# Linear-attention layers: the query feature's minimum on GpSimd, and the attention's last step as one VectorE operation per quarter of the channels

## What is computed

```python
def _feature_map(x):
    return jax.nn.elu(x) + 1.0
for i in range(B):                       # B = 8 layers
    residual = x
    Q = _feature_map(jnp.einsum('nsd,hdk->nshk', x, Wq[i]) + bq[i])
    Kf = _feature_map(jnp.einsum('nsd,hdk->nshk', x, Wk[i]) + bk[i])
    V = jnp.einsum('nsd,hdk->nshk', x, Wv[i]) + bv[i]
    KV = jnp.sum(Kf * V, axis=1)
    sumK = jnp.sum(Kf, axis=1)
    Z = 1.0 / (Q * sumK[:, None] + 1e-06)
    att = Q * KV[:, None] * Z
    att = att.reshape(n, s, H * K)
    y = jax.nn.gelu(att @ Wo[i] + bo[i])
    x = _layer_norm(y + residual, ln1_s[i], ln1_b[i])
    residual = x
    h = jax.nn.gelu(x @ W1[i] + b1[i])
    h = jax.nn.gelu(h @ W2[i] + b2[i])
    x = _layer_norm(h + residual, ln2_s[i], ln2_b[i])
```

## Time and profile before

| what | value |
|---|---|
| median of 3 runs | 3349.62 us (3346.64 to 3351.68) |
| the profiled execution | 3358.28 us |
| its span | 3356.5 us |
| TensorE busy | 2989.0 us, 89% of the span |
| VectorE busy | 2665.6 us, 79% |
| ScalarE busy | 2443.9 us, 73% |
| GpSimd busy | 843.9 us, 25% |
| mean granted TensorE clock | 0.944 |

### The profile page before, as it was taken

How to read it: one execution, slowest core, us unless ns; L and a number is a source line. 1 busy time by engine, 2 the same in 40 slices (tenths; PEclk the granted TensorE clock), 3 DMA queues, 4 the chain that set the end, 5 groups by cost and what they waited for, 6 DMA issues and landing times. The chain is left out here.

```text
span 3356.5 us, 51221 instructions
## 1 busy us (share of the span) xinstructions
PE 2989.0 (89%) x14363; PEld 1985.1 (59%) x14368; DVE 2665.6 (79%) x10483; ACT 2443.9 (73%) x4542; POOL 843.9 (25%) x1000
## 2 busy tenths in 40 slices
PE   6999998172599999999999999999999999999767
PEld 5777776161456666666666666666666666666444
DVE  4656665753489999988999999899999999898647
ACT  5888886031478888888888888788888888888643
POOL 2444444283111121111112112112111211121126
PEclk9999998586699999999999999999999999999868
DMA  1000000222100000000000000000000000000000
GB/s 54 1 0 0 0 0 14 100 34 38 64 1 1 20 13 1 20 7 8 1 25 8 1 20 7 8 12 15 7 1 20 13 1 1 1 1 1 1 7 26
DMA packets 31563, 46.34 MB, mean 14 GB/s; under 512 B 5315, under 2 KB 21731, under 8 KB 31334
## 3 DMA queue, kind: packets, MB, share of 16 engines
q1 hardware_dynamic: 25702, 39.46, 3.5%
q0 software_dynamic: 5632, 4.20, 0.9%
HBM read 35.16 MB, written 8.49 MB: 13 GB/s over the span
## 5 line engine op out<-in xcount | busy, mean ns | idle before, releaser
L1774 DVE TENSOR_SCALAR t_feat_q<-t_recip,t_neg_mean 128x256 f32<-128x256 f32 x1024 | 400.8, 453 | 112.4 <-ACT t_recip L1634 109.4
L1480 PE MATMUL t_o_ps<-t_feat_q,t_wo 128*128 128x512 f32 x1024 | 474.5, 596 | 6.8 <-issue 4.1
L1626 ACT ACTIVATE t_recip<-t_feat_q,t_z_scale 128x256 f32<-128x256 f32 x1024 | 434.8, 499 | 1.7 <-DVE t_feat_q L1774 1.0
L1612 ACT ACTIVATE t_exp_k<-t_k_ps 128x1024 f32<-128x1024 f32 x256 | 259.8, 1015 | 233.4 <-PE t_k_ps L1457 233.4
L1737 DVE CUSTOM_DVE_ANT_0 t_junk<-t_v_ps,t_feat_k 128x256 f32<-128x256 f32 x1024 | 390.7, 419 | 8.2 <-PE t_v_ps L1457 8.0
L1727 DVE SCALAR_TENSOR_TENSOR t_feat_k<-t_exp_k,t_k_ps 128x256 f32<-128x256 f32 x1024 | 369.4, 417 | 21.4 <-ACT t_exp_k L1612 21.4
L1898 POOL TENSOR_TENSOR t_var_eps<-t_moments,t_ln_eps 128x4 f32<-128x4 f32 x128 | 69.3, 542 | 1240.2 <-DVE t_moments L1785 1240.2
L1616 ACT ACTIVATE t_exp_q<-t_q_ps 128x1024 f32<-128x1024 f32 x256 | 261.7, 1022 | 87.1 <-PE t_q_ps L1457 86.3
L1763 DVE SCALAR_TENSOR_TENSOR t_feat_q<-t_exp_q,t_q_ps 128x1024 f32<-128x1024 f32 x256 | 312.7, 1222 | 8.8
L1480 PEld LDWEIGHTS t_o_ps<-t_feat_q,t_wo 128*128 128x128 f32 x1024 | 194.5, 190 | 180.9 <-issue 160.0
L243 POOL TENSOR_TENSOR a_probs<-a_probs,a_inv 128x256 f32<-128x256 f32 (+1 forms) x256 | 209.3, 839 | 274.5 <-DVE a_inv L340 274.5
(11 more groups left out here) (370 smaller groups left out, 7424.5 us busy)
## 6 DMA issues: line engine op xcount, KB each, us to landing
t_raw_w<-in_wk SPq DMA_DIRECT2D x8, 512.0 KB, 3.7
t_raw_w<-in_wq SPq DMA_DIRECT2D x8, 512.0 KB, 4.6
t_raw_w<-in_wv SPq DMA_DIRECT2D x8, 512.0 KB, 5.4
t_raw_o<-in_wo SPq DMA_DIRECT2D x8, 512.0 KB, 3.7
t_raw<-in_w SPq DMA_DIRECT2D x16, 256.0 KB, 2.7
x<-in_x SPq DMA_DIRECT2D x4, 512.0 KB, 6.9
tokens_dram<-r_hn SPq DMA_DIRECT2D x8, 256.0 KB, 2.3
e_w_raw<-in_fc_w SPq DMA_DIRECT2D x4, 512.0 KB, 3.8
```

Of the source, the lines that this page charges most:

```text
L1480: last = pe.matmul(o_ps[:], wo[:, chunk, :], feat_q[:, s, chunk, :], start=(chunk == 0), stop=(chunk == NC - 1), skip_group_check=True)
L1612: act.activation(exp_k[:], k_ps[:], ACT.Exp, bias=-1.0).then_inc(c["k_exp"], 1)
L1626: last = act.activation(recip[:, q % 2, k * UNIT + n * SEQ:k * UNIT + (n + 1) * SEQ], feat_q[:, s, chunk, cols], ACT.Ln, bias=1.0, scale=z ...
L1774: last = dve.tensor_scalar(feat_q[:, s, chunk, cols], recip[:, q % 2, k * UNIT + n * SEQ:k * UNIT + (n + 1) * SEQ], -1.0, neg_mean[:, s, n ...
```

## The change

The minimum of the query feature goes from VectorE to GpSimd (`less_one`): the carrier waits for the exponential, the minimum follows and raises `q_less_one`, for which VectorE's feature waits as before. The four calls of a step stand between GpSimd's other work. The attention's last step becomes one operation over a quarter of the channels, which are two chunks for two batches: it reads `recip` and, as a second tensor, `neg_mean` spread over the 256 tokens; for that `neg_mean` is laid out with the batch innermost.

```diff
-        neg_mean = sb("t_neg_mean", [P, 2, 2, NC])
+        neg_mean = sb("t_neg_mean", [P, 2, NC, 2])
...
-                dve.scalar_tensor_tensor(neg_mean[:, s, :, :], kv_all[:], -1.0, inv_sum[:], ALU.mult, ALU.mult).then_inc(c["kv_ready"], 1)
+                dve.scalar_tensor_tensor(neg_mean[:, s, :, :].rearrange("p c n -> p n c"), kv_all[:], -1.0, inv_sum[:], ALU.mult, ALU.mult).then_inc(c["kv_ready"], 1)
 
             def feature_q(t, s, q):
-                dve.wait_ge(c["q_exp"], 4 * t + q + 2)
-                dve.tensor_scalar(exp_q[:], exp_q[:], 1.0, -1.0, ALU.min, ALU.add).then_inc(c["q_less_one"], 1)
                 dve.wait_ge(c["q_less_one"], 4 * t + q + 2)
...
-                for k in range(2):
-                    for n in range(2):
-                        chunk, cols = 2 * q + k, slice(n * SEQ, (n + 1) * SEQ)
-                        last = dve.tensor_scalar(feat_q[:, s, chunk, cols], recip[:, q % 2, k * UNIT + n * SEQ:k * UNIT + (n + 1) * SEQ],
-                                                 -1.0, neg_mean[:, s, n, chunk:chunk + 1], ALU.add, ALU.mult)
-                last.then_inc(c["att_ready"], 1)
+                means = neg_mean[:, s, 2 * q:2 * q + 2, :].rearrange("p c n -> p (c n)").unsqueeze(2).broadcast_to([P, 4, SEQ])
+                dve.scalar_tensor_tensor(feat_q[:, s, 2 * q:2 * q + 2, :].rearrange("p c (n t) -> p (c n) t", n=2),
+                                         recip[:, q % 2, :].rearrange("p (a t) -> p a t", t=SEQ), -1.0, means,
+                                         ALU.add, ALU.mult).then_inc(c["att_ready"], 1)
...
+            def less_one(t, q):
+
+                pool.wait_ge(c["q_exp"], 4 * t + q + 2)
+                carry(3)
+                pool.tensor_scalar(exp_q[:], exp_q[:], 1.0, -1.0, ALU.min, ALU.add).then_inc(c["q_less_one"], 1)
...
+                if A:
+                    less_one(t, 0)
                 if closing is not None:
                     pool.wait_ge(c["o_filled"], 4 * (t - 2) + 5)
                     swap_wo(closing)
+                if A:
+                    less_one(t, 1)
                 if E:
                     rstd_of(t - 4, 1, c["stats2_ready"], c["var2_ready"], c["rstd2_ready"])
+                if A:
+                    less_one(t, 2)
                 if C:
                     rstd_of(t - 2, 0, c["stats1_ready"], c["var1_ready"], c["rstd1_ready"])
-                if active(at, 0) and at != UNITS - 1:
+                if A and at != UNITS - 1:
                     split_x(t + 1, r)
+                if A:
+                    less_one(t, 3)
```

More of the change, by code:

```diff
@@ L1909, in step @@
                 s, r = at % 2, 1 - at % 2
-                C, Dn, E = (active(at, k) for k in (2, 3, 4))
+                A, C, Dn, E = (active(at, k) for k in (0, 2, 3, 4))
                 if at == 0:
```

## The result

The changed kernel takes 3831.86 us (median of 4 runs, 3827.47 to 3832.99). The kernel before took 3348.13 us on the same chip (4 runs, 3345.82 to 3351.68). The ratio is 1.1441, with a 95% interval of 1.1421 to 1.1461: slower by 484 us, or 14.4%. The forecast was slower by 39 us, and by some 80 at most.

What follows compares the result with a forecast made beforehand. TensorE's list and its bias-group waits for the query feature were taken to bound the kernel; 57 times 0.62 = 35.3 us plus 3.7 us of filling gave +39, from 3349.6 to 3389 us, range 3370 to 3430 us.

Steps and rivals of the forecast that it cites:

- What bounds the kernel: In the layer stack, TensorE's list plus its waits, chiefly 64 bias-group waits for the query feature, 43.4 us in all.
- The price of the minimum: GpSimd's minimum taken as 1.05 us, making the path from exponential to feature 1.38 us instead of 0.76.
- GpSimd's minimum is dear: Rival: at 2.56 us the chain grows 1.5 us more and the first quarter pays too; 3475 to 3500 us; chance 0.07.
- Three other quarters: In a unit's other three quarters the longer path costs nothing while about 0.33 us of spare time lasts.
- The sum: 57 waits times 0.62 plus 3.7 us of filling: +39 us, median 3389 us; chance of 3375 to 3403 us 0.66.
- The port between the two engines: Rival: GpSimd and VectorE lock each other out; a further lost turn adds 45 us, 3434 us; 3403 to 3440: 0.15.
- The attention's last step: On VectorE, four operations of 256 columns become one of 1024, about 1.18 us; TensorE does not wait for it; priced zero.
- the seven units with copies: Units with 1.47 us waits behind weight copies gain 1.13 and pay 0.62 us each; put at zero, 4 us either way.
- The filling: As the pipeline fills, six bias groups wait for a key feature behind a query feature: 6 times 0.62, +3.7 us.

Runs made afterwards that it cites:

- The multiply: The whole change with GpSimd's minimum replaced by a multiplication by 1e-30, same addition, place and waits, feature values not those wanted: 3395.84 us, ratio 1.0138.
- the probe: The kernel before, with twelve GpSimd operations on 128x1024 fp32 tiles ahead of the stack, other engines waiting: minimum-add and other pairs 3.63 to 3.65 us.
- quarters 0 to 2 alone: The change with the minimum on GpSimd for quarters 0 to 2 only, back on VectorE for quarter 3: 3563.92 us, ratio 1.0644.

## Why the prediction was wrong

**What bounds the kernel**: right. The bias group of quarter 0 waits for the feature of quarter 3, and what is put into that chain goes into each step once. The multiply shows it with 0.62 us forecast and 0.65 measured, the changed kernel with 3.14 in the path and 3.13 in the wait.

**The price of the minimum**: the step that failed. The prediction bounded it by "the one-input row of 1.05 us is of the same shape and the nearest, and I take it" and 2.56 us as the upper end. It took 3.63. The row was of the same shape and the same number of inputs but of another pair of operations, and in the probe the price hangs on the pair. The upper end failed for the same reason: in the probe an operation with one input and two steps costs more than one with two inputs. The Trainium skill's "GPSIMD Engine Reference" (section Engine selection), by which one-input work is roughly line rate, comes near for multiply-add alone (1.05 us). For the minimum the trace has 3.63 us, some 3.5 times that, and the measurement decides. So "GpSimd's minimum is dear" was the rival that came true, with a chance of 0.07 and a time, 3475 to 3500 us, that is some 340 us too low.

**Three other quarters that cost nothing "as long as the spare time lasts"**: the condition was right and its consequence not carried through. The spare time was 0.33 us, and with a path of 3.90 the three together cost 216 us when they are moved alone. In the rival of the dear minimum only "the first quarter pays as well"; quarters 0 and 1 both pay, through the values and through the bias group of quarter 2; behind quarter 2's feature no wait grew.

**The sum had no term for the clock.** With 3.63 put into its own scheme, 57 waits of 0.08 + 0.20 + 3.63 + 0.05 − 0.76 = 3.20 us give 182 us, and quarters 0 to 2, measured alone, another 216, together some 400 of the 484. The matmuls at the lower level behind the long waits add some 120, and some 48 come off again because the values wait less than in quarters 0 to 2 alone. No row of the kernel before showed a wait that long in a plain unit, so its rows gave no price for this.

**The port between the two engines**: as forecast, without cost worth a term. The two engines do hold each other up: in the multiply's kernel GpSimd's split takes 2.29 us beside an attention step, and the next attention step 1.64 instead of 1.23 beside the multiply. But the plain waits are 0.99 us, and the other quarters are not held.

**The attention's last step and the seven units with copies**: priced at zero and 0 ± 4 us. The step alone gives 3.5 us back (its interval ends just short of no change); in the multiply's kernel the waits of 1.47 us have gone with the rest to 0.99 or 1.45. **The filling**: +3.7 us forecast; in the multiply's kernel the six bias groups wait 5.2 us for the key feature, not 4.6, so +0.6. Its time is 47.5 us above that of before, 8.5 us above the sum of 39, while between the two profiled executions the span grew by 40.8 only. The profiled execution of before, whose rows the sum was made of, stood 8.7 us above its median; where a usual execution is that much shorter, no trace shows, and so the 8.5 us stay open.

## What to carry to other kernels

A price taken from the nearest row must be of the same operation, not only of the same engine, shape and number of inputs; where the trace has no such row, a probe of a few lines on the chip settles what no bound from other rows can. When a step that feeds the bounding engine grows by several times, work the sum again for all its repeats and not for the one that was critical, since the spare time of the others is fixed. And a long wait of TensorE may cost more than its length: look at the granted clock in short windows behind it.

## What the hardware showed that was not expected

- GpSimd on 1024 columns of fp32: multiply-then-add 1.05 us; minimum-add, maximum-add, add-add and multiply-minimum 3.63 to 3.65; a minimum or an addition alone 2.77 and 2.78; two tensors 2.34.
- At each of TensorE's waits of some 3.5 to 3.9 us its granted clock fell to 0.50, in some units while it still stood idle, in others within 2 us after it worked again, and stayed there for some 3.5 to 4 us or for some 7; at waits of 0.99 or 1.21 us it stayed at 1.00. Matmuls in the place of the long wait kept it at 1.00 but for three places, and brought 57 us.
- One VectorE operation of 1024 columns was held up less by GpSimd's run of copies (2.12 us) than four of 256 columns (3.45 us), though its undisturbed length is greater (1.23 against 1.14).
